# Expanding the first block of up weights inside the attention stage, and keeping the first split input

## Time and profile before

| | us |
|---|---|
| median of 3 runs | 1819.6 (1816.1 to 1820.48) |
| profiled execution, its time | 1812.74 |
| profiled execution, its span | 1811.0 |
| PE busy | 1673.6 (92%) |
| DVE busy | 1211.1 (67%) |
| ACT busy | 383.6 (21%) |
| POOL busy | 610.9 (34%) |
| DMA read from HBM | 157.45 MB |

### The profile page before, as it was taken

The page is one execution under the profiler, slowest core; times in us unless marked ns, Lnnn a source line. Parts: engine busy times, 40 slices in busy tenths (PEclk is TensorE's granted clock), DMA queues, the critical chain, the costliest instruction groups (busy, mean ns, idle before and its releaser), DMA issues. The chain is left out here.

```text
span 1811.0 us, 21282 instructions
## 1 busy us (share of the span) xinstructions
PE 1673.6 (92%) x7024; PEld 1188.9 (66%) x7024; DVE 1211.1 (67%) x1801; ACT 383.6 (21%) x654; POOL 610.9 (34%) x451
## 2 busy tenths in 40 slices
PE   6899946999999999969999999999997799999996
PEld 3343425646656566448888888888885467888885
DVE  6999845778778888555447787777775666242413
ACT  1222220111111110122213222322321222121211
POOL 3587612454564456431012222322321332000101
PEclk9999978999999999989999999999998899999998
DMA  5534467766666756231300000000003433201011
GB/s 192 190 133 174 156 199 224 220 222 208 219 205 203 242 186 224 82 128 47 105 12 15 21 24 12 24 12 24 13 24 121 124 99 117 76 29 64 29 41 35
DMA packets 87621, 202.60 MB, mean 112 GB/s; under 512 B 7280, under 2 KB 29552, under 8 KB 79472
## 3 DMA queue, kind: packets, MB, share of 16 engines
q1 hardware_dynamic: 87536, 201.52, 33.5%
HBM read 157.45 MB, written 44.04 MB: 111 GB/s over the span
## 5 line engine op out<-in xcount | busy, mean ns | idle before, releaser
L986 POOL TENSOR_TENSOR r_rS<-r_S,r_rT 128x512 f32<-128x512 f32 x128 | 184.0, 1440 | 207.8 <-DVE r_S L1079 207.5
L1679 POOL TENSOR_TENSOR l_sq<-l_expq,l_reluq 128x512 f32<-128x512 f32 x64 | 83.1, 1299 | 373.3 <-ACT l_expq L1863 373.3
L1770 DVE SCALAR_TENSOR_TENSOR l_acc<-l_ps,l_inv,l_acc 128x512 f32<-128x512 f32 x240 | 166.6, 749 | 30.6 <-PE l_ps L703 30.5
L1079 DVE TENSOR_TENSOR_SCAN r_S<-r_dT,r_ps 128x512 f32<-128x512 f32 x128 | 156.4, 1222 | 17.3 <-POOL r_rS L986 13.2
L2197 DVE CAST g_x_part<-g_x 128x512 fp32r<-128x512 f32 x64 | 38.8, 606 | 186.5 <-ACT g_x L2255 186.5
L1430 PE MATMUL r_ps<-Wdn,r_h 128*128 128x512 f32 x352 | 154.6, 595 | 0.0
L1430 PEld LDWEIGHTS r_ps<-Wdn,r_h 128*128 128x128 f32 x352 | 65.7, 190 | 85.5 <-issue 85.4
L701 PE MATMUL g_ps<-g_x_part,g_Wup 128*128 128x512 f32 x256 | 102.5, 400 | 12.5 <-DVE g_x_part L2185 9.8
L2127 POOL TENSOR_TENSOR g_xs<-g_xs,relay 128x512 f32<-128x512 f32 x16 | 21.8, 1360 | 265.0 <-DVE relay L2178 253.2
L701 PE MATMUL l_ps<-l_M_part,l_sq_part 128*128 128x512 f32 x256 | 106.9, 418 | 2.8 <-DVE l_sq_part L1786 2.8
L701 PE MATMUL g_ps<-g_Wdn,g_x_part 128*128 128x512 f32 x256 | 103.8, 406 | 0.0
(11 more groups left out here) (221 smaller groups left out, 3731.8 us busy)
## 6 DMA issues: line engine op xcount, KB each, us to landing
r_w_part<-scratch_wgu SPq DMA_DIRECT2D x28, 1024.0 KB, 7.1
r_V<-scratch_v SPq DMA_DIRECT2D x96, 256.0 KB
first_part<-scratch_wgu SPq DMA_DIRECT2D x16, 1024.0 KB, 6.5
relay<-scratch_x SPq DMA_DIRECT2D x12, 1024.0 KB, 6.3
scratch_wgu<-f_halves SPq DMA_DIRECT2D x28, 384.0 KB, 4.4
...
```

The lines of the kernel that those rows point to most:

```text
L986: nc.gpsimd.tensor_tensor(rS[u % RS][:, :], S[u % 2][:, 0:T], rT[u // DK][:, :], ALU.mult).then_inc(rS_ready.sem, 1)
L1079: nc.vector.tensor_tensor_scan(S[u % 2][:, 1:T + 1], dT[hh][:, :], kv, 0.0, ALU.mult, ALU.add).then_inc(S_ready.sem, 1)
L1679: nc.gpsimd.tensor_tensor(sq[i % 2][:, :], expq[i % 2][:, :], reluq[i % 2][:, :], ALU.add).then_inc(sq_ready, 1)
L1770: last = nc.vector.scalar_tensor_tensor(acc[b][:, t, :], ps, inv[i % 2][:, t:t + 1], acc[b][:, t, :], ALU.mult, ALU.add)
```

## The change

A set of buffers `kept` now lives from the attention stage into the feed-forward: the high and low part of up block 0 (`up`), the high and low part of x^T of batch 0 (`x_part`), the block's scales (`scale`) and the low-rank factor `narrow` with its parts.

- In the attention's first half the plain copy of x^T of batch 0 and its store are gone. Its split parts stay for the feed-forward. SP loads `narrow`, `low_rows` and the scales of block 0 behind the wide factors.
- In units 31 to 34 ScalarE casts the factors (`high_factor`), and VectorE makes their parts at the end of the next unit (`factor`).
- Behind units 44, 46, 48 and 50 TensorE has one job `lora` each. In the next unit VectorE expands the tile (`expand`) between `minimum` and `accumulate` of the sums, and ScalarE casts its high part (`high_up`) behind the copy of M; GpSimd makes its low part (`low_up`) one unit later.
- At the end of the attention SP loads x^T of batch 1 (not 0) and the integers of block 1.
- The feed-forward begins with up block 0 and the split x of batch 0 in place: its semaphores are advanced by the same counts, and the instructions are gone. Its first loads are reordered.

```diff
+    HIGH_AT = [31 + n for n in range(I1 // C)]
+    LORA_AT = [44 + 2 * kt for kt in range(KT)]
...
             jobs += [("q", i), ("M", i)]
         if i >= LATE:
             jobs += [("norm", i - LATE)] + [("head", i - LATE, t) for t in range(TT)]
+        if i in LORA_AT:
+            jobs += [("lora", LORA_AT.index(i))]
...
+        xT = kept["xT"]
+        x_part = [kept["x_part"]] + [[sb(f"x_part{i}{b}", [P, KT, T], F32R) for i in range(2)] for b in range(1, B)]
+        wide, wide_hi, factors = relay[1], kept["up"][1], parts[1]
+        low_rows = sb("low_rows", [P, 2])
+        narrow_hi = sb("narrow_hi", [P, C], F32R)
+        narrow, narrow_part = kept["narrow"], kept["narrow_part"]
+        up_q, up_scale = relay[0][:, :, :].bitcast(I32), kept["scale"]
+        whole = [bkv["k"], bkv["v"]]
...
             def store_xT(b):
-                sp.wait_ge(xT_ready, (b + 1) * KT)
+                sp.wait_ge(xT_ready, b * KT)
                 sp.dma_start(slab(spill["x2"], b), flat(xT[:, :, :])).then_inc(xT_stored, 16)
...
             sp.wait_ge(wkv_lo_ready["k"], KT)
             load_x(1)
-            store_xT(0)
             sp.wait_ge(*product("xT", 0, KT - 1))
...
-            sp.dma_start(relay[0][:, :, :].bitcast(I32), w["up_q"].rearrange("p (k c) -> p k c", k=KT)[:, :, 0:C]).then_inc(
-                hand, 16)
+            sp.dma_start(up_q, w["up_q"].rearrange("p (k c) -> p k c", k=KT)[:, :, 0:C]).then_inc(up_loaded, 16)
             store_xT(3)
             sp.wait_ge(*product("xT", 3, KT - 1))
-            sp.dma_start(flat(relay[1][:, :, :]), w["g_wide"]).then_inc(hand, 16)
+            sp.dma_start(flat(wide[:, :, :]), w["g_wide"]).then_inc(wide_loaded, 16)
+            sp.dma_start(narrow[:, :], w["g_narrow"]).then_inc(narrow_loaded, 16)
+            sp.dma_start(low_rows[:, :], w["low_rows"]).then_inc(narrow_loaded, 16)
+            for a in range(2):
+                sp.dma_start(up_scale[64 * a:64 * a + 64, :],
+                             w["up_scale"][:, 0:C].unsqueeze(1).broadcast_to([8, 8, C])).then_inc(narrow_loaded, 16)
             for h in range(2, QH):
                 load_raw(h)
-            sp.wait_ge(xT_stored, 16 * B)
+            sp.wait_ge(xT_stored, 16 * (B - 1))
             sp.wait_ge(w_lo_ready, QH)
-            sp.dma_start(flat(relay[2][:, :, :]), slab(spill["x2"], 0)).then_inc(hand, 16)
+            sp.dma_start(flat(relay[2][:, :, :]), slab(spill["x2"], 1)).then_inc(hand, 16)
+            sp.wait_ge(expanded, 2 * KT - 1)
+            sp.dma_start(up_q, w["up_q"].rearrange("p (k c) -> p k c", k=KT)[:, :, C:2 * C]).then_inc(hand, 16)
             for b in range(B):
...
+            def low_up(kt):
+                pool.wait_ge(up_hi_ready, kt + 1)
+                pool.wait_ge(factor_ready, 1 + I1 // C)
+                nc.gpsimd.tensor_tensor(kept["up"][1][:, kt, :], whole[kt % 2][:, :],
+                                        kept["up"][0][:, kt, :].bitcast(F32), ALU.subtract).then_inc(up_lo_ready, 1)
             low_kv("k", 0)
             low_kv("k", 1)
...
+                if i - 2 in LORA_AT:
+                    low_up(LORA_AT.index(i - 2))
         @block.vector
...
+            def factor(n):
+                if n == 0:
+                    dve.wait_ge(narrow_hi_ready, 1)
+                    nc.vector.scalar_tensor_tensor(narrow_part[:, :], narrow_hi[:, :].bitcast(F32), low_rows[:, 1:2],
+                                                   narrow[:, :], ALU.mult, ALU.add).then_inc(factor_ready, 1)
+                dve.wait_ge(wide_hi_ready, n + 1)
+                nc.vector.scalar_tensor_tensor(factors[:, n, :], wide_hi[:, n, :].bitcast(F32), low_rows[:, 0:1],
+                                               wide[:, n, :], ALU.mult, ALU.add).then_inc(factor_ready, 1)
+            def expand(kt):
+                if kt == 0:
+                    dve.wait_ge(up_loaded, 16)
+                if kt >= 2:
+                    dve.wait_ge(up_lo_ready, kt - 1)
+                nc.vector.scalar_tensor_tensor(whole[kt % 2][:, :], up_q[:, kt, :], -7.5, up_scale[:, :], ALU.add,
+                                               ALU.mult).then_inc(expanded, 1)
+                dve.wait_ge(expanded, 2 * kt + 1)
+                dve.wait_ge(*product("lora", kt))
+                nc.vector.tensor_tensor(whole[kt % 2][:, :], whole[kt % 2][:, :], place("lora", kt)[:, :],
+                                        ALU.add).then_inc(expanded, 1)
             statistics(0)
...
             for i, (h, b) in enumerate(units):
                 minimum(i, h)
+                if i - 1 in LORA_AT:
+                    expand(LORA_AT.index(i - 1))
...
                 low_M(i)
                 split_sq(i)
+                if i - 1 in HIGH_AT:
+                    factor(HIGH_AT.index(i - 1))
             accumulate(UNITS - 1, *units[-1])
...
             def copy_x(b):
-                if b > 0:
-                    act.wait_ge(xT_stored, 16 * b)
+                if b > 1:
+                    act.wait_ge(xT_stored, 16 * (b - 1))
                 for kt in range(KT):
                     act.wait_ge(*product("xT", b, kt))
-                    nc.scalar.activation(xT[:, kt, :], place("xT", b, kt)[:, :], ACT.Copy).then_inc(xT_ready, 1)
+                    if b > 0:
+                        nc.scalar.activation(xT[:, kt, :], place("xT", b, kt)[:, :], ACT.Copy).then_inc(xT_ready, 1)
                     nc.scalar.activation(x_part[b][0][:, kt, :], place("xT", b, kt)[:, :], ACT.Copy).then_inc(x_hi_ready, 1)
...
+            def high_factor(n):
+                if n == 0:
+                    act.wait_ge(narrow_loaded, 4 * 16)
+                    nc.scalar.activation(narrow_hi[:, :], narrow[:, :], ACT.Copy).then_inc(narrow_hi_ready, 1)
+                    act.wait_ge(wide_loaded, 16)
+                nc.scalar.activation(wide_hi[:, n, :], wide[:, n, :], ACT.Copy).then_inc(wide_hi_ready, 1)
+            def high_up(kt):
+                act.wait_ge(expanded, 2 * kt + 2)
+                if kt == 0:
+                    act.wait_ge(xT_stored, 16 * (B - 1))
+                nc.scalar.activation(kept["up"][0][:, kt, :], whole[kt % 2][:, :], ACT.Copy).then_inc(up_hi_ready, 1)
             act.wait_ge(handed, 3 * 16)
...
                 nc.scalar.activation(M_part[i % 2][0][:, :], place("M", i)[:, :], ACT.Copy).then_inc(M_hi_ready, 1)
+                if i in HIGH_AT:
+                    high_factor(HIGH_AT.index(i))
+                if i - 1 in LORA_AT:
+                    high_up(LORA_AT.index(i - 1))
...
+                elif kind == "lora":
+                    pe.wait_ge(factor_ready, 2)
+                    last = nc.tensor.matmul(out[:, :], narrow_part[0:3 * RANK, n * P:(n + 1) * P],
+                                            factors[0:3 * RANK, 0, :], start=True, stop=True)
...
+        def up_part(i, kt, at, width):
+            return kept["up"][i][:, kt, at:at + width] if at < C else Wup_rest[i][:, kt, at - C:at - C + width]
...
-            sp.dma_start(narrow[:, :], w["g_narrow"]).then_inc(narrow_loaded, 16)
-            sp.dma_start(low_rows[:, :], w["low_rows"]).then_inc(narrow_loaded, 16)
             sp.dma_start(b_up[:, :], w["b_up"]).then_inc(small_loaded, 16)
-            sp.dma_start(b_dn[:, :], w["b_dn"]).then_inc(small_loaded, 16)
-            sp.wait_ge(handed, 3 * 16)
-            sp.sem_inc(up_loaded, 16)
-            sp.sem_inc(xT_loaded.sem, 16)
+            load_up_scale(1)
             load_down(0)
             load_down_scale(0)
             load_down_scale(1)
-            load_up_scale(1)
+            sp.dma_start(b_dn[:, :], w["b_dn"]).then_inc(small_loaded, 16)
+            sp.wait_ge(handed, 2 * 16)
+            sp.sem_inc(up_loaded, 2 * 16)
+            sp.sem_inc(up_scale_loaded[0], 2 * 16)
+            sp.sem_inc(xT_loaded.sem, 2 * 16)
             for j in range(0, UT, 2):
                 if j % 4 == 0 and j // 4 + 1 < OB:
-                    load_up(j // 4 + 1)
+                    if j > 0:
+                        load_up(j // 4 + 1)
                     if j // 4 + 2 < OB:
                         load_up_scale(j // 4 + 2)
                 if j + 2 < UT:
                     load_down_scale(j + 3)
             sp.wait_ge(expanded, 2 * len(order))
-            with sp.Fori(1, B) as b:
+            finish(0)
+            with sp.Fori(2, B) as b:
...
         def _(pool):
             out_ready.ahead(pool)
+            pool.sem_inc(w_lo_ready, len(first_tiles))
             for i, x in enumerate(order):
-                part = Wup[1][:, x[2], x[1] * C:(x[1] + 1) * C] if x[0] == "up" else Wdn[1][:, x[1], :]
-                high = Wup[0][:, x[2], x[1] * C:(x[1] + 1) * C] if x[0] == "up" else Wdn[0][:, x[1], :]
+                if x in first_tiles:
+                    continue
+                part = up_part(1, x[2], x[1] * C, C) if x[0] == "up" else Wdn[1][:, x[1], :]
...
             def sequence(b, first):
```

(56 more changed lines are left out.)

45 lines of the change are left out of this document (19 added, 26 removed).

## The result

| kernel | median of its runs (us) | ratio to the kernel before, 95% interval |
|---|---|---|
| before | 1819.8 (1816.1 to 1820.5) | |
| after | 1799.8 (1796.2 to 1800.9) | 0.9896 [0.9878, 0.9914] |
| before, again | 1814.2 (1812.4 to 1821.5) | 0.9997 [0.9984, 1.001] |
| after, again | 1800.4 (1795.3 to 1801.1) | 0.9904 [0.9889, 0.9919] |

Faster by 1.0%: some 17 to 19 us by the two ratios, 20.0 between the first two medians, where 15.8 us and 1803.8 us were forecast (range 1797 to 1811.5). The profiled executions are only 13.5 us apart (spans 1811.0 and 1797.5), since that of the kernel before (1812.7) was quicker than all of its timed runs. From the start of each stage to that of the next, the stages ahead of the attention differ by +1.0 us, the attention by +3.65 (786.58 to 1401.21, against 785.57 to 1396.55), the feed-forward by -18.16 (396.29 against 414.45).

A forecast was written before the change was run, and what follows sets the result against it. PE bounds the attention's second half and the feed-forward's first batch, but idles at the border between them. Terms -17.7 + 2.1 - 0.2 = -15.8 us from the median 1819.6 give 1803.8 us; own range 1801.7 to 1807.1, wider 1797 to 1811.5.

The forecast's parts named there:

- The border: Between attention and feed-forward: first relu 17.7 us earlier (16.5 to 18.4), the fifth up product keeping its distance from it.
- the landing of the down scales: At the border: scales land 5.0 us after issue (earlier trace 4.8 to 6.2), so the down tile's expansion starts at 1404.4.
- the 12 that the prediction had named as its limit: Sign of a wrong forecast: third up product more than 12 us after the stage's end; some 10.5 expected.
- PE stands still no more after it: Feed-forward after the fifth up product: PE has no more halts, so what the border saves is saved for good.
- The weighed rule: Attention's expansions: two-SBUF-input VectorE instructions and GpSimd exclude each other; would lose 1 us in all, forecast 1804.8; left out.
- The attention: PE in the attention's second half: four `lora` products cost 0.52 us each, 2.1 us together (1.0 to 3.0).
- VectorE at nothing: Attention: VectorE's 9.0 us of additions in eight units cost nothing, with 0.8 us left in hand in the expansion units.
- the start at -0.2: Attention's start: ScalarE writes four tiles instead of eight, gaining 0.2 us (0 to 0.5) at the first k product.
- Rival 5: More gain: no low clock at the attention's end and start, scales landing early; -20.4 us, 1799.2, chance 0.05.
- Rivals 1 and 3: Attention: VectorE's additions reach PE in full, 1812.8, chance 0.07; late sq splits halt PE and drop the clock, 1830, 0.05.
- rival 4: Border: first product or relu waits for another thing until about the old time; +1.9 us, 1821.5, chance 0.04.
- Rival 2: Border: clock stays at 1.2 GHz until the fifth up product, gaining 10.2 instead of 17.7; -8.3, 1811.3, chance 0.06.

The follow-up runs named there:

- after_again: The changed kernel, unaltered, measured once more: 1800.4 us, ratio 0.9904 to the kernel before.
- after_resplit: The changed kernel, but the feed-forward's first batch splits an x again (batch 1's), and ScalarE's bias wait moves to the first relu: 1797.0 us, ratio 0.9912.
- before_again: The kernel before, unchanged, measured and traced once more: 1814.2 us, ratio 0.9997.
- the experiment: The changed kernel with three more VectorE expansion-like instructions in each of the four attention units that expand part of up block 0: 1806.4 us, ratio 0.994.
- after_x_shift: The changed kernel with 32 unused bytes ahead of and 32 behind the kept split x, no instruction changed: 1805.2 us, ratio 0.9935.
- before_aligned: The kernel before with 32 and 32 bytes of padding round the split x of both stages: 1818.6 us, ratio 1.0008.
- before_same256: The kernel before with unused bytes round the attention's x (160, 128) and ahead of the feed-forward's (160), for equal remainders modulo 256: 1795.9 us, ratio 0.9896.

## Why the prediction was right, step by step

**The border, forecast -17.7.** It gave -15.3 by the fifth up product, and the mechanism held: no factor, x or block 0 instruction is left there, and PE starts 0.46 us after the stage's end (0.2 to 0.5 forecast). The term is 2.4 us too large. Step that was mis-sized: the landing of the down scales. Forecast was the expansion of the down tile 7.85 us after the stage's end; it came after 9.16 (1410.37 - 1401.21), though the second half of the scales was issued 2.87 us after it (1403.47 + a quarter of the row's 2.45, less 1401.21), as forecast (2.85). So the landing took 6.2 to 6.3 us, where I had chosen 5.0 and the earlier trace rows ended at 6.2. The 5.0 rested on the tile's scales being among the first of the four, but both halves must be in, and of the four it was the second that took the 6.2 us, before as after. This costs 1.3 us (9.16 for 7.85). In the other kernels the same transfer, issued at the same place of the list, took 5.3 to 7.2 us, so a share of such a figure is chance. Issues and landings in 1401 to 1407 (median us in the last column):
```profile
g_xs<-in_dn_q SPq DMA_DIRECT2D x1, 512.0 KB, 6.4
g_tanh_z<-in_dn_scale SPq DMA_DIRECT2D x4, 128.0 KB, 5.2
g_b_dn<-in_b_dn SPq DMA_DIRECT2D x1, 256.0 KB, 6.1
```
The integers, too, took 6.4 us where the earlier trace rows had 4.3 to 6.0. The second part is the wait on `b_dn`, which I had read as an item of SP's list but not as one of ScalarE's waits: the change moved that transfer to the end of the list, and a wait on the count of two transfers waits for the later one. From the down tile's expansion to the relu it is 2.74 us where I had put 1.98, so 0.76 more. The third product stood 12.6 us after the stage's end, beyond the 12 that the prediction had named as its limit; it was past it for these causes. The fifth kept 17.8 us from the relu (17.42 forecast): 1.3 + 0.76 + 0.4 are the 2.4 us. That PE stands still no more after it, which was to save the gain for good, held in part: at the first products of blocks 2 and 3 PE waits 0.35 and 0.53 us for GpSimd's low parts, where the kernel before has no such hole. These holes vary: 2.4 us in after_again, none in after_resplit, 0.7 in before_again.

**The weighed rule.** At 1414.36 VectorE's difference with two SBUF inputs took 1.67 us instead of 0.69, GpSimd's starting at 1414.00: the Trainium skill (SBUF — State Buffer, "Who interferes with whom") has it so, and the trace agrees. In the attention the four expansions met no GpSimd work (681 to 683 ns each), as I had read from the earlier trace rows; the extra ones of the experiment did.

**The attention, forecast +2.1, VectorE at nothing and the start at -0.2.** The eight units from the first `lora` took 59.09 us against 57.13 for eight without: +1.96 for four. PE never waited for VectorE in units 32 to 52. In hand were 0.8 us, by the experiment's trace as by the forecast. At the attention's start nine k matmuls took 2.40 us instead of 2.63, as forecast.

**What the prediction didn't have.** Two terms. The placing of the operands: by the table, up 768 x 5.0, q -0.5, k and v -0.7, heads -0.5, M +0.4, down -0.2, together -5.2 us; after_x_shift, which takes it from batch 0 and up, costs 0.9935 against 0.9904, 5.6 us. Against it +2.4 us for the low clock of the attention's first units, which all kernels but before and before_again show (first unit 4.9 to 6.4 us long against 3.6); why is open. The moved work is not needed for it: before_aligned and before_same256, in which only places were moved, show it too in their one trace each (6.0 and 5.6 us).

Sum: -15.3 + 2.0 - 5.2 + 2.4 = -16.1 us, against -13.5 between the profiled executions and -17.4 from after_again's ratio (1816.8 x 0.0096). Of the 2.6 us between the sum and the profiled executions 1.0 lies ahead of the attention, where nothing was changed, 0.9 are the two new holes of PE, and the rest has no cause that I know. The forecast of -15.8 came out near it partly because an error of 2.4 and the clock's 2.4 stood against 5.2 that no step of mine contained. Without the accident of the places the change would have been worth about 11 us by this sum; after_x_shift, which lacks most of it, has 11.8 (1815.75 x 0.0065). Rival 5 (1799.2) has the nearest number and the wrong reason: there was more low clock, not less. Rivals 1 and 3 fell with VectorE's rows and rival 4 with the relu, which comes 15.6 us earlier after the stage's end. Rival 2's clock fell again for 3 us at the border, which costs some 1.5 us, not 8.
